# State-space stage: C products of three states on GpSimd, B in quarters, decays in three PSUM banks

## The reference, cut to what matters

```python
def _selective_scan(u, dt, A, Bm, Cm, Dp):
    def step(h, inp):
        u_t, dt_t, B_t, C_t = inp
        dA = jnp.exp(dt_t[:, :, None] * A)
        h = dA * h + (dt_t * u_t)[:, :, None] * B_t[:, None, :]
        y = jnp.einsum('bds,bs->bd', h, C_t)
        return (h, y)
    ...
    return ys.transpose(1, 0, 2) + u * Dp

def _mamba(x, Win, convw, convb, Wx, Wdt, bdt, Alog, Dp, Wout):
    xi, z = jnp.split(x @ Win, 2, axis=-1)
    xi = jax.nn.silu(_causal_dwconv(xi, convw, convb))
    xdbc = xi @ Wx
    dt_in, Bm, Cm = ...
    dt = jax.nn.softplus(dt_in @ Wdt + bdt)
    y = _selective_scan(xi, dt, -jnp.exp(Alog), Bm, Cm, Dp)
    return y * jax.nn.silu(z) @ Wout
...
yf = _layernorm(_mamba(x, ...) + x, ...)
yb = _layernorm(flip(_mamba(flip(x), ...)) + x, ...)
y = yf + yb
return _layernorm(relu(y @ ff_W1 + ff_b1) @ ff_W2 + ff_b2 + y, ...)
```

## Time and profile before

| | us |
|---|---|
| median of 3 runs | 5596.02 (5586.29 to 5598.56) |
| the profiled execution | 5577.15 |
| its span, first to last instruction | 5575.1 |
| VectorE busy in the span | 4512.3 (81%) |
| TensorE matmuls busy | 4029.1 (72%) |
| GpSimd busy | 3140.3 (56%) |
| ScalarE busy | 2779.2 (50%) |

### The profile page before, as it was taken

The page is one execution under the profiler, slowest core; times in us unless marked ns, Lnnn a source line. Parts: engine busy times, 40 slices in busy tenths (PEclk is TensorE's granted clock), DMA queues, the critical chain, the costliest instruction groups (busy, mean ns, idle before and its releaser), DMA issues. The chain is left out here.

```text
span 5575.1 us, 103824 instructions
## 1 busy us (share of the span) xinstructions
PE 4029.1 (72%) x29177; PEld 2314.7 (42%) x29180; DVE 4512.3 (81%) x8773; ACT 2779.2 (50%) x6405; POOL 3140.3 (56%) x3422
## 2 busy tenths in 40 slices
PE   5777778777777787774777748887283888689943
PEld 2333233332333333332455536666283666456621
DVE  5999999999999999996898877776246777667778
ACT  3545555455555554552677734445374455345434
POOL 6877777777777777775565643324544222233302
PEclk8999989988998999987888869997696888799965
DMA  2111111011101110111545526666115555366511
GB/s 82 65 52 48 67 67 67 36 65 67 66 33 67 67 67 36 65 65 28 100 87 86 94 55 107 112 110 166 48 60 118 96 101 95 67 114 119 104 40 30
DMA packets 320172, 420.38 MB, mean 75 GB/s; under 512 B 40000, under 2 KB 301712, under 8 KB 309136
## 3 DMA queue, kind: packets, MB, share of 16 engines
q1 hardware_dynamic: 315536, 408.35, 31.4%
q0 software_dynamic: 4352, 8.95, 0.5%
HBM read 307.65 MB, written 109.58 MB: 75 GB/s over the span
## 5 line engine op out<-in xcount | busy, mean ns | idle before, releaser
L2184 POOL TENSOR_TENSOR m_h<-m_dtu,m_Bb 128x512 f32<-128x512 f32 x1024 | 1589.5, 1582 | 229.3 <-PE bank L1819 223.1
L1819 PE MATMUL bank<-m_h,ident 128*128 128x512 f32 x2048 | 1211.3, 682 | 500.1 <-DVE m_h L2083 487.2
L1819 PEld LDWEIGHTS bank<-m_h,ident 128*128 128x128 f32 x2048 | 362.0, 206 | 1163.3 <-DVE m_h L2083 1014.9
L2077 DVE TENSOR_TENSOR_SCAN m_h<-m_dA,m_h 128x512 f32<-128x512 f32 x512 | 750.5, 1466 | 6.3 <-DVE m_sz L2010 6.3
L2083 DVE TENSOR_TENSOR m_h<-m_h,bank 128x512 f32<-128x512 f32 x1024 | 674.2, 659 | 5.2 <-issue 3.4
L2077 DVE TENSOR_TENSOR_SCAN m_h<-bank,m_h 128x512 f32<-128x512 f32 x512 | 621.3, 1214 | 27.9 <-DVE m_sz L2010 11.9
L1966 ACT ACTIVATE bank<-m_dt,m_A 128x512 f32<-128x512 f32 x512 | 352.3, 688 | 495.6 <-DVE m_h L2077 435.5
L1966 ACT ACTIVATE m_dA<-m_dt,m_A 128x512 f32<-128x512 f32 x512 | 367.2, 717 | 429.4 <-DVE m_h L2077 425.6
L516 ACT ACTIVATE x_sm<-x_sm,x_nm 128x77 f32<-128x77 f32 x1024 | 353.5, 349 | 113.3 <-DVE x_nm L679 112.9
L861 POOL TENSOR_TENSOR x_sm<-x_sm,x_gp 128x308 f32<-128x308 f32 x256 | 219.5, 860 | 132.3 <-ACT x_sm L516 132.3
L377 PE MATMUL bank<-ident,x_sm 128*77 128x128 f32 x1024 | 195.9, 322 | 134.5 <-DVE x_pT L702 121.5
(11 more groups left out here) (422 smaller groups left out, 10560.0 us busy)
## 6 DMA issues: line engine op xcount, KB each, us to landing
m_Bb<-m_B SPq DMA_DIRECT2D x32, 4096.0 KB, 12.0
x_Ks<-x_k_parts SPq DMA_DIRECT2D x32, 462.0 KB
x_q_parts<-x_qp SPq DMA_DIRECT2D x32, 384.0 KB, 4.0
x_Qs<-x_q_parts SPq DMA_DIRECT2D x32, 384.0 KB
f_Ks<-f_k_parts SPq DMA_DIRECT2D x16, 768.0 KB
a_Ks<-a_k_parts SPq DMA_DIRECT2D x16, 768.0 KB
x_xp<-x_stage SPq DMA_DIRECT2D x32, 256.0 KB
x_Qs<-x_q_parts SPq DMA_DIRECT2D x32, 256.0 KB
```

The costliest lines, as they stand in the source:

```text
L1819: pe.matmul(banks[4 + c], ident[:], h[:, k % RING, :], start=(s == 0), stop=(s == NS - 1)).then_inc(s_ya.sem, 1)
L2077: v.tensor_tensor_scan(h[:, k % RING, :], decays[k % AHEAD], h[:, k % RING, :], 0.0, ALU.mult, ALU.add).then_inc(s_h.sem, 1)
L2184: pool.tensor_tensor(h[:, k % RING, :], dtu[:, d, c, :], Bb[:, d, s, :], ALU.mult).then_inc(s_dB.sem, 1)
```

## The change

- Decays go to three banks (0, 1, 3) in turn; `AHEAD` is 3, the two SBUF tiles are gone.
- All C spreads go to bank 2. A spread waits for the last product that VectorE made before it.
- The products of states 2, 6 and 10 (six slots a unit) are made by GpSimd: SyncE stores C as well, reads back three of its rows spread over the partitions (`Cb`), and GpSimd multiplies h by them, `BEHIND` = 4 slots after its input of the slot. These states have no spread on TensorE.
- `Bb` holds one unit, in four quarters; each is refilled when GpSimd has used it in the unit before.
- `RING` 16 instead of 8, `LAG` 4 instead of 2; the pieces o:1 and o:2, the steps y, o_stats and gated move to later slots.

The diff, without the hunks that only declare semaphores:

```diff
@@ -1495,9 +1495,15 @@
     SL = NS * NC
-    RING = 8
-    LAG = 2
-    AHEAD = 4
+    RING = 16
+    LAG = 4
+    BEHIND = 4
+    AHEAD = 3
+    QUARTERS, QS = 4, NS // 4
+    BY_POOL = (2, 6, 10)
+    BY_DVE = tuple(s for s in range(NS) if s not in BY_POOL)
+    AT_DVE, AT_POOL = {s: n for n, s in enumerate(BY_DVE)}, {s: n for n, s in enumerate(BY_POOL)}
+    BY_QUARTER = [[s for s in BY_POOL if s // QS == j] for j in range(QUARTERS)]
     TURNS = NG // 2
@@ -1547,7 +1553,7 @@
-    PE_AT = ({0: ["xT"], 1: ["c0:0"], 2: ["c0:1", "o:0", "c0:2"], 7: ["o:1", "c0:3"], 8: ["o:2"], 10: ["z0"], 11:
+    PE_AT = ({0: ["xT"], 1: ["c0:0"], 2: ["c0:1", "o:0", "c0:2"], 7: ["c0:3"], 8: ["o:1"], 9: ["o:2"], 10: ["z0"], 11:
               ["c1:0", "c1:1", "c1:2", "c1:3"], 14: ["xd:0", "xd:1", "z1"], 16: ["dt0"], 18: ["dt1"], 21: ["yT:0"],
@@ -1557,10 +1563,10 @@
                "xd"], 22: ["dt0"], 23: ["dt1"], 24: ["exp"], 26: ["log", "o"], 31: ["move", "o_norm"]})
-    DVE_AT = ({0: ["y"], 11: ["o_stats"], 14: ["z0", "u"], 16: ["z1"], 23: ["split", "e"], 30: ["dtu"]},
-              {2: ["y", "f_stats"], 8: ["f_affine"], 13: ["u", "z0"], 15: ["z1"], 22: ["e"], 25: ["split", "o_stats"],
+    DVE_AT = ({3: ["y"], 12: ["o_stats"], 14: ["z0", "u"], 16: ["z1"], 23: ["split", "e"], 30: ["dtu"]},
+              {2: ["f_stats"], 4: ["y"], 8: ["f_affine"], 13: ["u", "z0"], 15: ["z1"], 22: ["e"], 25: ["split", "o_stats"],
                28: ["dtu"]})
-    POOL_AT = ({4: ["gated"], 15: ["o_pow"], 31: ["dt", "far"]},
+    POOL_AT = ({6: ["gated"], 15: ["o_pow"], 31: ["dt", "far"]},
                {8: ["f_pow"], 13: ["out_pow"], 14: ["gated"], 26: ["dt"], 30: ["o_pow"], 31: ["far"]})
@@ -1614,11 +1621,11 @@
         Cs = sb("Cs", [CROW + NS, 2, GT], BF16)
-        Bb = sb("Bb", [P, 2, NS, GT])
+        Bb = sb("Bb", [P, NS, GT])
+        Cb = sb("Cb", [P, len(BY_POOL), GT])
         dt = sb("dt", [P, 2, NC, GT])
...
         h = sb("h", [P, RING, GT])
-        dA = sb("dA", [P, AHEAD - 2, GT])
         yd = sb("yd", [P, NC, GT])
@@ -1649,8 +1657,8 @@
         turned_by = (ident, flip)
-        convw = Bb[:, 0, 0:4, :].rearrange("p a t -> p (a t)")
-        decays = (banks[0], dA[:, 0, :], banks[1], dA[:, 1, :])
+        convw = Bb[:, 0:4, :].rearrange("p a t -> p (a t)")
+        decays = (banks[0], banks[1], banks[3])
         block = st.enter_context(nc.Block())
@@ -1691,14 +1699,26 @@
+            def spread(n, d, j):
+                lo = QS * j
+                sp.wait_ge(s_dB.sem, s_dB.at(n - 1, NC * (lo + QS)))
+                sp.sem_inc(s_step, 1)
+                sp.dma_start(Bb[:, lo:lo + QS].rearrange("p s t -> p (s t)"),
+                             Bd[d, lo:lo + QS].rearrange("s t -> (s t)").rearrange("(a n) -> a n", a=1).to_broadcast([P, QS * GT])).then_inc(s_Bb[j].sem, 16)
+                for row in BY_QUARTER[j]:
+                    at = AT_POOL[row]
+                    sp.wait_ge(s_hP.sem, s_hP.at(n - 1, NC * (at + 1)))
+                    sp.sem_inc(s_step, 1)
+                    sp.dma_start(Cb[:, at], Cd[d, row:row + 1].to_broadcast([P, GT])).then_inc(s_Cb[j].sem, 16)
+
             def spread_B(n, g, d):
...
                 sp.sem_inc(s_step, 1)
-                sp.wait_ge(s_dB.sem, s_dB.at(n - 1))
                 sp.dma_start(Bd[d], xd[BROW:BROW + NS, :]).then_inc(s_Bd.sem, 16)
+                sp.dma_start(Cd[d], xd[CROW:CROW + NS, :]).then_inc(s_Bd.sem, 16)
                 sp.wait_ge(s_Bd.sem, s_Bd.at(n + 1))
-                sp.dma_start(Bb[:, d].rearrange("p s t -> p (s t)"),
-                             Bd[d].rearrange("s t -> (s t)").rearrange("(a n) -> a n", a=1).to_broadcast([P, NS * GT])).then_inc(s_Bb[d].sem, 16)
+                for j in range(QUARTERS - 1):
+                    spread(n, d, j)
@@ -1718,11 +1738,13 @@
                     g = 2 * i + l
+                    spread(2 * g, 0, QUARTERS - 1)
                     spread_B(2 * g + 1, g, 1)
...
                         load(g + 1, 1 - l)
+                    spread(2 * g + 1, 1, QUARTERS - 1)
                     if not (first and not l):
@@ -1805,17 +1827,20 @@
             def spread_C(n, d, s):
-                if s == 0:
+                if s == BY_DVE[0]:
                     pe.wait_ge(s_Cs.sem, s_Cs.at(n + 1))
                     pe.wait_ge(s_Csh.sem, s_Csh.at(n + 1))
-                pe.wait_ge(s_hC.sem, s_hC.at(n, 2 * s - 2))
-                pe.matmul(banks[2 + s % 2], selC[:, s, :], Cs[:, d, :], start=True, stop=True).then_inc(s_C.sem, 1)
+                pe.wait_ge(s_hC.sem, s_hC.at(n, NC * AT_DVE[s]))
+                pe.matmul(banks[2], selC[:, s, :], Cs[:, d, :], start=True, stop=True).then_inc(s_C.sem, 1)
...
                     pe.wait_ge(s_yd.sem, s_yd.at(n - 1, c + 1))
-                pe.wait_ge(s_hC.sem, s_hC.at(n, k + 1))
+                if s in AT_POOL:
+                    pe.wait_ge(s_hP.sem, s_hP.at(n, NC * AT_POOL[s] + c + 1))
+                else:
+                    pe.wait_ge(s_hC.sem, s_hC.at(n, NC * AT_DVE[s] + c + 1))
                 pe.matmul(banks[4 + c], ident[:], h[:, k % RING, :], start=(s == 0), stop=(s == NS - 1)).then_inc(s_ya.sem, 1)
@@ -1836,7 +1861,7 @@
                         add(n - 1, SL - LAG + k)
-                    if k % 2 == 1 and k // 2 + 1 < NS:
+                    if k % 2 == 1 and k // 2 + 1 in AT_DVE:
                         spread_C(n, d, k // 2 + 1)
@@ -1962,7 +1987,7 @@
                     act.wait_ge(s_dt.sem, s_dt.at(n + 1))
-                act.wait_ge(s_h.sem, s_h.at(n, k + 1 - AHEAD))
+                act.wait_ge(s_h.sem, s_h.at(n, k + 1 - AHEAD if k >= AHEAD else max(j for j in range(1 - AHEAD, 1) if (j + SL - 1 - k) % AHEAD == 0)))
                 act.activation(decays[k % AHEAD], dt[:, d, c, :], ACT.Exp, scale=A[:, d, c, s:s + 1]).then_inc(s_dA.sem, 1)
@@ -2078,9 +2103,11 @@
                 s = k // NC
+                if s in AT_POOL:
+                    return
                 v.wait_ge(s_h.sem, s_h.at(n, k + 1))
-                v.wait_ge(s_C.sem, s_C.at(n, s + 1))
-                v.tensor_tensor(h[:, k % RING, :], h[:, k % RING, :], banks[2 + s % 2], ALU.mult).then_inc(s_hC.sem, 1)
+                v.wait_ge(s_C.sem, s_C.at(n, AT_DVE[s] + 1))
+                v.tensor_tensor(h[:, k % RING, :], h[:, k % RING, :], banks[2], ALU.mult).then_inc(s_hC.sem, 1)
@@ -2177,11 +2204,21 @@
                 s, c = k // NC, k % NC
-                if k == 0:
-                    pool.wait_ge(s_Bb[d].sem, s_Bb[d].at(g + 1))
+                if k % (NC * QS) == 0:
+                    pool.wait_ge(s_Bb[s // QS].sem, s_Bb[s // QS].at(n + 1))
                     pool.sem_inc(s_step, 1)
                 pool.wait_ge(s_ya.sem, s_ya.at(n, k + 1 - RING))
-                pool.tensor_tensor(h[:, k % RING, :], dtu[:, d, c, :], Bb[:, d, s, :], ALU.mult).then_inc(s_dB.sem, 1)
+                pool.tensor_tensor(h[:, k % RING, :], dtu[:, d, c, :], Bb[:, s, :], ALU.mult).then_inc(s_dB.sem, 1)
+
+            def times_C(n, k):
+                s, c = k // NC, k % NC
+                if s not in AT_POOL:
+                    return
+                if c == 0 and s == BY_QUARTER[s // QS][0]:
+                    pool.wait_ge(s_Cb[s // QS].sem, s_Cb[s // QS].at(n + 1))
+                    pool.sem_inc(s_step, 1)
+                pool.wait_ge(s_h.sem, s_h.at(n, k + 1))
+                pool.tensor_tensor(h[:, k % RING, :], h[:, k % RING, :], Cb[:, AT_POOL[s], :], ALU.mult).then_inc(s_hP.sem, 1)
@@ -2200,6 +2237,8 @@
                     inputs(2 * g + d, g, d, k)
+                    if k >= BEHIND:
+                        times_C(2 * g + d, k - BEHIND)
                     for what in side(POOL_AT, g, d, k):
```

More of the change, by code:

```diff
@@ L1586, in mamba @@
         Bd = nc.dram_tensor("m_B", (2, NS, GT), F32, kind="Internal").ap()
+        Cd = nc.dram_tensor("m_C", (2, NS, GT), F32, kind="Internal").ap()
         flip = sb("flip", [P, P])
@@ L1637, in mamba @@
         s_hi = sem("C_hi"); s_mid = sem("C_mid"); s_Cs = sem("C_lo"); s_Csh = sem("C_moved", 2)
-        s_Bd = sem("B_stored", 16); s_Bb = [sem(f"B_spread{d}", 16) for d in range(2)]
+        s_Bd = sem("B_and_C_stored", 32); s_Bb = [sem(f"B_spread{j}", 16) for j in range(QUARTERS)]
+        s_Cb = [sem(f"C_rows_spread{j}", 16) for j in range(QUARTERS)]
         s_ab = sem("abs", 4); s_z = sem("exp_abs"); s_w1 = sem("one_plus"); s_ln = sem("log"); s_e = sem("correction")
         s_d1 = sem("log_corrected"); s_dr = sem("dt_raw"); s_dtu = sem("dtu"); s_dt = sem("dt")
-        s_C = sem("C_spread", NS); s_dA = sem("decay", SL); s_dB = sem("input", SL); s_h = sem("state", SL)
-        s_hC = sem("state_C", SL); s_ya = sem("summed", SL); s_yd = sem("y_D", 2); s_yz = sem("y_gated")
+        s_C = sem("C_spread", len(BY_DVE)); s_dA = sem("decay", SL); s_dB = sem("input", SL); s_h = sem("state", SL)
+        s_hC = sem("state_C", NC * len(BY_DVE)); s_hP = sem("state_C_by_pool", NC * len(BY_POOL)); s_ya = sem("summed", SL); s_yd = sem("y_D", 2); s_yz = sem("y_gated")
```

## The result

The changed kernel takes 5802.24 us (median of 4 runs, 5787.47 to 5811.26) against 5591.66 for the kernel before, run beside it: ratio 1.0373 [1.0347, 1.0400], 211 us. The forecast was 5662 in 5485 to 5730: right in its sign, far too small in its size, and outside the range.

The account below looks back on a forecast made before the run. VectorE was taken to pace the state-space stage; per pair of units, costs 21.1 less gains 16.8 made 4.3 us slower, 69 us over 16 pairs, carried to the median 5665, forecast 5662 us, range 5485 to 5730.

Parts of the forecast that it names:

- The gains: On VectorE, per pair of units: scans with all decays in banks save 8.1 us, three states' products moved away 6.9.
- y: Direction 0, slot 3: VectorE's y step waits for the add of product 31, behind the gate; 3.4 us a pair.
- steps 1 and 4: Direction 0: VectorE waits for decay 2 behind xT, 1.8 us a pair, and for decay 30 behind m1, 1.3.
- e: Direction 1, slot 22: VectorE waits for ScalarE's exp, which starts later with three decays ahead; 2.5 us a pair.
- GpSimd: Direction 0: gating of the late y holds GpSimd before input 10, where VectorE needs short slots; 0.8 us a pair.
- u: Direction 0, slot 14: VectorE waits for ScalarE's chain from decay 16 to c1's end; 1.1 us a pair.
- z0 and z1: Direction 1: these steps lose 0.9 us a pair because ScalarE starts later with three decays ahead.
- Step 3: Direction 1, slot 2: VectorE's f_stats waits for TensorE's f pieces behind the gate and ScalarE's copy; 3.3 us a pair.
- With TensorE free at the gate the spread itself costs nothing: Gate: a C spread's wait for VectorE's last product; the spread was to be done 0.6 us before it is wanted.
- the clock term: TensorE: some of chains xT, y, f_stats and m1 run at 1.2 GHz instead of 2.4; 0.5 us a pair taken.
- the split: Four small VectorE instructions splitting C, held by GpSimd: 4.0 us a pair more in d = 0 (with e), 1.5 in d = 1.
- GpSimd as the bound: Rival: GpSimd's 12 products at 1.22 us set the pace, 7.7 us a pair more, 5785 us; chance 6%.

Follow-up runs that it names:

- the repeat: The changed kernel itself, unedited, measured again in a later session: 5781.77 us, 1.0368 of the kernel before.

## Why the prediction was right in its sign and wrong in its size

**The gains** (8.1 + 6.9 us a pair) came as counted: scans 1371.8 to 1230.8 us, products 674.2 to 550.8.

**Where the miss is.** In the stage VectorE's busy time was forecast to change by 16 x (5.5 - 15.0) = -152 us and its idle time by 16 x (15.1 + 0.5 - 1.8) = +221. Measured are -167 and +353. The busy side was right; 132 us of waiting are missing, and 105 of them are one row. The sign came from stalls that were there, but the margin was thin, 21.1 against 16.8 us a pair. (The forecast 5662 is also 3 us under the prediction's own sum, 5665; that changes nothing.)

**The named stalls** came at the places named, and mostly in size. Over 16 pairs, forecast and measured in the stage: y 54 and 55; decays behind xT and m1 (steps 1 and 4) 50 and 53; e 40 and 32; GpSimd 13 and 25; u 18, measured 22 above the 9 of before. z0 and z1, forecast 14, are twice that, 29 above 29. Step 3, the f statistics, was 53 and is 62: single waits are 3.2 us, as forecast, or 4.8.

**The step that failed** is the sentence "With TensorE free at the gate the spread itself costs nothing", with its 0.6 us to spare, and the clock term of 0.5 us a pair that stood for all slow stretches. Measured: 105.4 us, 6.6 a pair. TensorE is not free at the gate, because it has waited at the one before, with the adds and pieces of the slots in between behind it. At 2.4 GHz it makes that up; at 1.2 GHz an add takes 1.83 us, more than VectorE's plain slot of 1.71 and far more than a short one of 1.14, so it makes up nothing. And I took the granted clock as given by the stage before, 0.90: it fell with the change. What lowered it stays open. TensorE's idle time in the stage went from 2498.4 - 1905.3 = 593 to 735 us, but idle time alone doesn't order the runs: with state 8 on GpSimd it is 734 us and the clock 0.89, with three decays ahead alone 567 us and 0.87, against 593 and 0.91 in the kernel before. No run changed the clock by itself. Before, spreads two slots ahead were the reserve that let slow stretches pass unseen.

**The gain of the shorter slots** was counted alone. The prediction had the cost of GpSimd's products under the port (5.5 us a pair, 88 in all); measured are 48 us in the split and 28 in the residual sum, which I had not named, and none in e. The total is near, 76 for 88, but by luck in part, since the places differ. By direction the split was forecast to go from 3.3 to 6.4 us in d = 0 and to grow by 1.5 in d = 1. It went from 3.2 to 5.2 in d = 0, and from 6.4 to 7.5 in d = 1. With all products on VectorE, the rest of the change kept, it takes 2.2 us in d = 0 and the same 7.5 in d = 1. So the products on GpSimd cost 3.0 us a pair in d = 0, which is the 48 us, and nothing in d = 1. There the one bank and the three decays had made it longer: with two banks, four decays and all products on VectorE it takes the 6.4 us of the kernel before. In d = 1 the trace shows who holds whom, VectorE first, then GpSimd:

```profile
1043.01 1.77 DVE L2044 CAST m_C_hi<-m_xd 16x512 bf16<-16x512 f32 x1
1044.82 2.72 DVE L2046 TENSOR_TENSOR m_C_rest<-m_xd,m_C_hi 16x512 f32<-16x512 f32 x1
1047.57 1.37 DVE L2048 CAST m_C_mid<-m_C_rest 16x512 bf16<-16x512 f32 x1
1048.97 1.63 DVE L2050 TENSOR_TENSOR m_Cs<-m_C_rest,m_C_mid 16x512 bf16<-16x512 f32 x1
```

```profile
1042.15 2.35 POOL L2187 TENSOR_TENSOR m_tu<-m_tu,m_cc 128x1024 f32<-128x1024 f32 x1 [5.48 <-ACT m_tu L1947]
1044.58 2.40 POOL L2189 TENSOR_TENSOR m_dt<-m_tu,m_tz 128x1024 f32<-128x1024 f32 x1
```

The subtraction of L2046 starts inside the second dt multiply, which ends at 1046.98, and ends 0.56 us after it; the same instruction takes 0.68 us when nothing holds it.

What was missing is the other end: a shorter slot can bring VectorE sooner to results of TensorE and ScalarE that are not there yet. The run with all products on VectorE shows that waits and held instructions together take all of the 110 us (192 x 0.575) back and 53 more; 84 us of that is idle time. None of the rivals foresaw this. The one nearest by its time, GpSimd as the bound (5785), is not what happened: GpSimd is busy 1854 of 2685 us in the stage.

**The rest of the program** was taken as fixed; it grew by 47 us in the profiled run and by 35 in the repeat. That is a quarter to a third of the 140 us between forecast and result.

**The sum, from the kernels' own ratios.** From 5579 us: ring, lag, quarters and moved steps -4 (0.9994); one C bank and three decays in banks +145 (1.0252), of which 132 are the order of the pieces behind the gate; the products on GpSimd +66 (to 1.0370). The +145 is a net figure: between those two runs the scans got 144 us shorter (1387.8 to 1243.5), and VectorE's idle time in the stage grew by 279 us (94.7 to 373.5). The one bank in the kernel before, whose decays stayed where they were, made it grow by 216 us (105.2 to 320.7). So no run shows that the deeper lag and the later y soften the gate.

## What to carry to other kernels

A buffer dropped in front of an engine that works in order is not a wait of its own reader alone: price the whole list from one gate to the next at the slow clock too, and try other work ahead of the gate. When work is taken off the pacing engine, ask for each result it reads whether it is there by the earlier time; slots are worth only as much as the slack of the others. And elementwise work moved to GpSimd can come back in the pacing engine's smallest instructions, here 48 us in four of them a unit: look at their durations, not at the busy share.
